# Two graph layers on one core: the mask products of TensorE in four column tiles of 32 instead of one of 128

## What is computed

```python
h = jnp.maximum(_layernorm(x, axis=-1), 0.0)
# layer 0: graph attention
scores = (Wh @ a1)[:, None] + (We @ a2)[None, :]         # Wh = h @ W, We = V @ W
e = jnp.where(scores > 0, scores, 0.2 * scores)
e = jnp.where(adj > 0, e, NEG_BIG)
attention = jax.nn.softmax(e, axis=1)
x = x + elu(attention @ V + h)
# layer 1: mean over neighbours
h = jnp.maximum(_layernorm(x, axis=-1), 0.0)
x = x + relu((adj.T @ h) @ U.T / adj.sum(axis=0)[:, None])
```

## Time and profile before

| | |
|---|---|
| median of three runs | 417.88 us |
| the profiled execution | 418.52 us, span of its instructions 416.3 us |
| TensorE, matmuls | 370.8 us busy (89%), 4797 |
| VectorE | 299.5 us (72%) |
| ScalarE | 278.3 us (67%) |
| GpSimd | 119.2 us (29%) |
| mask products, line 1088 | 88.0 us busy, 1056 |
| products with V, line 1110 | 129.1 + 17.8 us, 1144 + 136 |
| products with the ones, line 1118 | 76.1 us, 960 |
| granted TensorE clock | 0.986 of full, mean |

### The profile page before, as it was taken

The page is one execution under the profiler, slowest core; times in us unless marked ns, Lnnn a source line. Parts: engine busy times, 40 slices in busy tenths (PEclk is TensorE's granted clock), DMA queues, the critical chain, the costliest instruction groups (busy, mean ns, idle before and its releaser), DMA issues.

```text
span 416.3 us, 11000 instructions
## 1 busy us (share of the span) xinstructions
PE 370.8 (89%) x4797; PEld 219.9 (53%) x4797; DVE 299.5 (72%) x425; ACT 278.3 (67%) x336; POOL 119.2 (29%) x120
## 2 busy tenths in 40 slices
PE   1618876889999999999999999999999999999996
PEld 0613544644444544444544445453444447999996
DVE  6799999898986848999848997832787563307333
ACT  2303867898899998888888988898999981110000
POOL 8870487782218502103202210220111100310000
PEclk9977999999999999999999999999999999999999
DMA  9999999999999999700000000000000000001100
GB/s 168 125 107 108 111 104 110 108 108 109 106 102 103 107 104 102 80 2 0 3 0 2 2 2 2 2 2 2 2 2 2 2 2 2 2 2 31 38 20 20
DMA packets 17946, 20.85 MB, mean 50 GB/s; under 512 B 13710, under 2 KB 13774, under 8 KB 17899
## 3 DMA queue, kind: packets, MB, share of 16 engines
q0 software_dynamic: 4752, 16.90, 39.0%
q1 hardware_dynamic: 10987, 2.70, 3.6%
q10 hardware_dynamic: 2160, 0.56, 0.7%
HBM read 69.79 MB, written 1.05 MB: 170 GB/s over the span
## 4 chain that ended last, share of the span: by engine, by line
PE 56%; DVE 18%; ACT 15%; issue 9%; DMA 1%; POOL 1%; ACTq 0%; DVEq 0%; POOLq 0%
PE w L1110 17%; PE q L1088 11%; PE q L1222 10%; DVE junk L776 9%; ACT arena L606 6%; ACT q L622 6%; PE den L1118 5%; PE w L1222 4%; DVE arena L819 4%; ACT arena L610 3%; PE w L1066 2%; PE den L1222 1%; PE w L995 1%; PE den L1131 1%; PE w L1180 1%
## 5 line engine op out<-in xcount | busy, mean ns | idle before, releaser
L776 DVE CUSTOM_DVE_ANT_0 junk<-adj_sb,t_row 125x2048 uint8<-125x2048 uint8 x66 | 154.9, 2348 | 2.1
L1110 PE MATMUL w<-arena,v_sb 128*32 128x500 f32 (+3 forms) x1144 | 129.1, 513 | 0.5 <-ACT arena L610 0.5
L622 ACT ACTIVATE q<-arena,minus_b 128x1000 f32<-128x1000 f32 (+2 forms) x114 | 106.1, 931 | 9.5 <-ACT arena L606 0.4
L1088 PE MATMUL q<-bi,adj_sb 128*128 128x125 bf16 x1056 | 88.0, 220 | 18.1 <-ACT q L622 16.1
L1088 PEld LDWEIGHTS q<-bi,adj_sb 128*128 128x128 fp8e4 x1056 | 61.8, 98 | 77.1 <-ACT q L622 42.5
L606 ACT ACTIVATE arena<-q,t_col 128x1000 f32<-128x1000 f32 (+2 forms) x106 | 94.6, 903 | 1.1 <-PE q L1088 0.7
L1118 PE MATMUL den<-arena,ones 128*32 128x250 f32 (+1 forms) x960 | 76.1, 339 | 0.0
L819 DVE SCALAR_TENSOR_TENSOR arena<-arena,b_col,q 128x1000 f32<-128x1000 f32 (+2 forms) x37 | 40.8, 1103 | 41.8 <-PE q L1088 34.3
L1118 PEld LDWEIGHTS den<-arena,ones 128*32 128x32 f32 x960 | 35.6, 110 | 51.6 <-issue 48.9
L610 ACT ACTIVATE arena<-arena,t 128x1000 f32<-128x1000 f32 (+2 forms) x37 | 37.2, 1006 | 21.9 <-DVE arena L819 21.7
L1222 PE MATMUL q<-g_all,adj_sb 124*124 124x129 f16 (+2 forms) x693 | 41.2, 220 | 0.0
(11 more groups left out here) (165 smaller groups left out, 338.8 us busy)
## 6 DMA issues: line engine op xcount, KB each, us to landing
adj_sb<-in_adj_dram POOLq DMA_DIRECT2D x33, 500.0 KB, 38.4
x_sb<-in_x_dram SPq DMA_DIRECT2D x1, 928.0 KB
out_dram<-x_sb SPq DMA_DIRECT2D x9, 84.0 KB
v_sb<-n_L_gnn_entity_embs_dram SPq DMA_DIRECT2D x2, 256.0 KB, 4.8
v_sb<-n_L_gnn_entity_embs_dram ACTq DMA_DIRECT2D x2, 256.0 KB, 5.7
out_dram<-x_sb SPq DMA_DIRECT2D x3, 56.0 KB
out_dram<-x_sb SPq DMA_DIRECT2D x9, 9.0 KB
x_sb<-in_x_dram SPq DMA_DIRECT2D x1, 125.0 KB
```

The lines of the kernel that those rows point to most:

```text
L622: nc.scalar.activation(part(q[n % Q_SLOTS], nb), a_part(nb), ACT.Relu, bias=minus_b[:, c:c + 1]).then_inc(relued, 1)
L776: nc.vector.tensor_tensor_reduce(out=junk[0:R, :], in0=adj_bytes[0:R, b, half], in1=t_row[0:R, half], scale=1.0 / ONE, scalar=0.0, op0=ALU ...
L1088: last = nc.tensor.matmul(q[n % Q_SLOTS][:, bank, start:start + R], adj_sb[:, b0 + k, c * P:(c + 1) * P], bi[:, i % BI_SLOTS, k, :], start ...
L1110: last = nc.tensor.matmul(att(i)[h * D + d:h * D + d + 32, 0:(k1 - k0) * R], v_sb[:, c, d:d + 32], e[:, k0 * R:k1 * R], start=first, stop= ...
```

## The change

Each mask product with 128 columns of weights becomes four with 32 columns, and each writes the 32 partitions of PSUM that its columns make. The moving operand, the accumulation flags and the semaphores stay. The further product of line 1094 is split in the same way. What is added up, and in which order, does not change for any element.

```diff
-                    last = nc.tensor.matmul(q[n % Q_SLOTS][:, bank, start:start + R],
-                                            adj_sb[:, b0 + k, c * P:(c + 1) * P], bi[:, i % BI_SLOTS, k, :],
-                                            start=not ON_ACT[n] and start == 0,
-                                            stop=ON_ACT[n] or (start == (in_bank - 1) * R and not again),
-                                            skip_group_check=ON_ACT[n])
-                    if again and start == (in_bank - 1) * R:
-                        last = nc.tensor.matmul(q[n % Q_SLOTS][:, bank, in_bank * R:4 * R],
-                                                adj_sb[:, b0 + k, c * P:(c + 1) * P], bi[:, i % BI_SLOTS, k, :],
-                                                start=False, stop=True)
+                    closes = start == (in_bank - 1) * R
+                    for e in range(0, P, 32):
+                        weights = adj_sb[:, b0 + k, c * P + e:c * P + e + 32]
+                        last = nc.tensor.matmul(q[n % Q_SLOTS][e:e + 32, bank, start:start + R], weights, bi[:, i % BI_SLOTS, k, :],
+                                                start=not ON_ACT[n] and start == 0, stop=ON_ACT[n] or (closes and not again),
+                                                skip_group_check=ON_ACT[n])
+                    if again and closes:
+                        for e in range(0, P, 32):
+                            weights = adj_sb[:, b0 + k, c * P + e:c * P + e + 32]
+                            last = nc.tensor.matmul(q[n % Q_SLOTS][e:e + 32, bank, in_bank * R:4 * R], weights,
+                                                    bi[:, i % BI_SLOTS, k, :], start=False, stop=True)
```

## The result

The changed kernel takes 421.74 us (median of 4 runs, 420.74 to 424.61) against 417.69 of the kernel before: a ratio of 1.0098, 95% interval 1.0071 to 1.0124. It is 4 us slower. The forecast was 405 us. 421.7 lies outside the 396 to 414 us that were most likely by the prediction, though inside the range, which was drawn up to 436 for the rivals' sake.

The account below looks back on a forecast made before the run. TensorE was taken to bound passes 2 to 5, ScalarE close behind and next to bind. Savings of 1.2 + 4.5 + 4.4 + 2.7 = 12.8 us from the 417.9 us median gave 405 us; 396 to 414 most likely, range 395 to 436.

Parts of the forecast that it names:

- Changes of shape and rounds: TensorE's tile: two shape changes of 0.08 to 0.11 us go, four mask products take 0.054; 0.20 us saved per 8-block tile.
- the other end: TensorE, from the products with the ones to the next mask: 0.53 us falls to 0.45, saving 0.08 a tile.
- Rival 2: Four mask products on TensorE take about 0.10 us, not 0.054, for their weight loads: +23 us, 441 us; chance 0.12.
- Part (e), the added instructions: TensorE's instruction queue: 6426 new instructions add 0.41 MB, 25 packets, nothing beside the adjacency's 16.90 MB unless a packet comes late.
- Rival 1: TensorE's instruction supply falls short in every pass, at most 29 ns each: up to 77 us more, 495 us; chance 0.14.
- The wait of 4 us for a pass: Passes 2 to 5: time beyond the busiest engine, then ScalarE, taken as 4 us each, leaving 12.8 us off.

Follow-up runs that it names:

- e5: Kernel before, with each mask product split into two column tiles of 64 in passes 4 and 5 only: 420.1 us, ratio 1.0036.
- e3: Changed kernel (split in all passes), with the adjacency of blocks 17 to 32 filled with ones on GpSimd instead of loaded: 412.44 us, ratio 0.9868.
- e11: Kernel before, split into four in passes 4 and 5, from chunk 16 of pass 3, and before that in every second tile of passes 2 and 3: 413.46 us.
- e4: Kernel before (mask of 128 in all passes), with the adjacency of blocks 17 to 32 filled with ones instead of loaded: 418.96 us, ratio 1.002.
- e2: Kernel before, with the masks split into four in passes 1 to 3 only: 426.92 us, ratio 1.0209.
- e9: Kernel before, split in passes 4 and 5 only, ScalarE tiles' exponentials there covering 600 of 1000 columns: 411.78 us, ratio 0.9856.
- e13: Kernel before, split in passes 4 and 5 only, VectorE's guards in pass 4 reading half of the columns: 413.4 us, ratio 0.9869.
- e15: Kernel before, split in passes 4 and 5 only, with half-column guards in pass 4 and 600-column exponentials in passes 4 and 5: 408.92 us, ratio 0.9755.

## Why the prediction was wrong

**Changes of shape and rounds: right in the main.** The 0.08 to 0.11 us for a change of shape carried over, and e5 shows that the shape was the gain. A steady tile gave back 0.10 + 0.11 = 0.21 us where 0.12 + 0.08 = 0.20 was summed. That the sum fits is in part luck, for a round takes 0.058 us and not 0.054, and the other end gave more than its 0.08. Over a whole pass less came: TensorE's busy time fell by 4.4 and 4.6 us in passes 2 and 3 (e3) and by 5.2 and 4.9 in passes 4 and 5, where 5.7 and three times 6.0 were summed. Rival 2 is refuted: 32 mask products in 0.46 us are 14 ns for each. The Trainium skill's floor of about 25 ns between starts ("TensorE: Matmul & The Clock Gate", Wait — 56ns, not 53.3ns?) is not met here, with four column tiles.

**Part (e), the added instructions: the step that failed.** It called 0.41 MB nothing beside the adjacency's 16.90 and left late packets to half a sentence. So it put at nothing a term that cost some 10 us. What counts is not the traffic that a packet adds but how late it starts among the loads: 3.4 to 4.1 us after TensorE had gone on with the one before, against 1.0 us when the loads were over. Rival 1 was the right mechanism, with a chance of 0.14, and priced wrongly: it took one rate for the whole kernel, between 3.5 and 29 ns, and looked for gaps in every pass. The runs show two regimes. Under the loads the supply gave 24.5 ns for an instruction where about 21.5 was asked (changed kernel), and sufficed at 27.7 (e11). Without them it sufficed at 21.5 (e3). The earlier trace rows had a sign of it, the DMA share of 1.02, 1.01 and 0.42 in passes 1 to 3, and the 96 instructions of a tile in 2.06 us (65.8 / 32, forecast for pass 3) would have asked for 21.4 ns; the trace of the kernel before doesn't show the limit itself.

Against e3 and e4 this cost the changed kernel 7.0 us in pass 2 (+6.0 where -1.0 was to be had) and 2.7 in pass 3 (+1.1 and -1.6). In the profiled execution a part of it is the clock: after the gap of 2.5 us at 135 us TensorE was granted 1.2 GHz for 3.4 us, and line 1066's 16 products took 3.14 us instead of 2.05:

```profile
137.50:141.00 3.50, 3.43 (x21) 2.52 (x21) 3.46 (x3) 0.89 (x1) 3.06 (x4) 0.56 1.01 105
```

```profile
139.05 3.14 PE L1066 MATMUL w<-ident,s 125*128 125x125 f32 x16
```

e2 had a gap of 2.5 us at nearly the same place and kept the full clock, and lost 4.9 us in pass 2 all the same.

**The wait of 4 us for a pass: too small.** The forecast was 1.2 + 4.5 + 4.4 + 2.7 us from passes 2 to 5. With the loads cut short (e3 against e4) they gave 1.0 + 1.6 + 1.6 + 2.1 = 6.3. Pass 2 and pass 5 came near, passes 3 and 4 fell short by 2.9 and 2.8. The term itself, the time of a pass beyond its busiest engine, measured 4.2 and 6.6 us in passes 2 and 3 (e3) and 6.2 and 3.7 in passes 4 and 5. The step took the sum of ScalarE's busy time for the bound. But ScalarE is late by stretches: for its own tiles it needs 2.20 us and TensorE 1.72, and in between it waits for VectorE. e9, e13 and e15 show both in pass 4. The 3.7 us that are left in e15 are open, and pass 3 was not tried.

**The sign.** The late packets cost some 10 us in passes 2 and 3 of the changed kernel, against the 6 that the split can give as the kernel stands. The two errors, 10 and 12.8 - 6.3 = 6.5 us, add up to the 16 to 17 us between forecast and result.

## What to carry to other kernels

Count instructions as well as work. Where a change multiplies an engine's instructions, work out the ns that it leaves for each, stretch by stretch, and look at the DMA share of the stretch: on this kernel about 21.5 ns was too little beside DMA engines with a share near 1 (one in 24.5 came), 27.7 was enough, and without the loads 21.5 was. A rewrite that is right for the array can then still be used where the loads are over (414.0 us), or in every second tile (413.5). And a gain on the bounding engine should be compared with the next engine's pace in a run of like tiles, not with its sum over a stage.

## What I had not expected of the hardware

- Four bf16 products of 125 columns with their own weight loads take 0.058 us together, no longer than one product with 128 columns of weights.
- TensorE went on 1.2 to 1.6 us after the end of the instruction packet it had lacked. So between the record of a packet and its use lies more than the packet's own 0.95 us.
- Two tiles of 64 beside tiles of 32 cost slightly more than one of 128: 0.5 and 0.7 us in a pass of 32 tiles (e5).
- Under the loads an instruction packet was late in starting and not slow in coming. Whether because the DMA engines are busy, because many loads are queued at once, or because of how GpSimd issues them, wasn't tried.
